# Windowed variance ratio on NHWC rows: 30 duos of raw boxes instead of 28, two of them around the mean, earlier warm-up, rings of two

## The reference

```python
def _gn(v, G=32, eps=1e-05):          # mean and variance of each group of 6 channels over one image
    g = v.reshape(B_, H_, W_, G, C_ // G)
    m = jnp.mean(g, axis=(1, 2, 4), keepdims=True)
    s = jnp.var(g, axis=(1, 2, 4), keepdims=True)
    return ((g - m) / jnp.sqrt(s + eps)).reshape(v.shape)

w0, w1, w2 = (1, 5, 20)
s = box_sum(box_sum(x, 1, w0), 2, w1)                         # sum of 5 along W
num = box_sum(s * s, 3, w2)                                   # sum of 20 along channels
d = box_sum(box_sum(box_sum(x * x, 1, w0), 2, w1), 3, w2)
denum = d * norm[None, :, :, None]                            # norm: how many of the 5 lie inside
ratio = nan_to_num(num / denum, nan=1.0)
```

## Time and profile before

| | |
|---|---|
| median of 3 runs | 393.49 us (393.3, 393.49, 395.51) |
| the profiled execution | 395.41 us, span 393.6 us |
| PE matmul busy | 371.3 us, 94% |
| ACT busy | 277.0 us, 70% |
| DVE busy | 262.5 us, 67% |
| POOL busy | 233.6 us, 59% |
| PE's share of the chain that ended last | 82% |

### The profile page before, as it was taken

How to read it: one execution, slowest core, us unless ns; L and a number is a source line. 1 busy time by engine, 2 the same in 40 slices (tenths; PEclk the granted TensorE clock), 3 DMA queues, 4 the chain that set the end, 5 groups by cost and what they waited for, 6 DMA issues and landing times.

```text
span 393.6 us, 8026 instructions
## 1 busy us (share of the span) xinstructions
PE 371.3 (94%) x3124; PEld 369.7 (94%) x3124; DVE 262.5 (67%) x555; ACT 277.0 (70%) x368; POOL 233.6 (59%) x150
## 2 busy tenths in 40 slices
PE   1999988999999999999889999999999999999982
PEld 1999988999999999999789999999999999999982
DVE  2999952676679999999766455445544455445544
ACT  1455549999999998996447667766777667766751
POOL 4000054887888888886088656765676556765431
PEclk9999989999999999999899999999999999999997
DMA  8999100588988952222203122222211222222213
GB/s 243 327 328 328 57 2 0 162 242 269 292 274 288 296 189 82 81 82 82 80 3 110 50 82 80 82 82 82 80 59 38 66 82 82 80 82 82 80 42 121
DMA packets 66485, 50.84 MB, mean 129 GB/s; under 512 B 912, under 2 KB 66448, under 8 KB 66448
## 3 DMA queue, kind: packets, MB, share of 16 engines
q1 hardware_dynamic: 66448, 50.34, 41.2%
HBM read 25.17 MB, written 25.17 MB: 128 GB/s over the span
## 4 chain that ended last, share of the span: by engine, by line
PE 82%; DVE 6%; issue 4%; ACT 4%; DMA 2%; POOL 0%; DVEq 0%; POOLq 0%; ACTq 0%
PE N L446 20%; PE U L437 19%; PE D L446 16%; PE S L437 16%; PE N L437 5%; PE S L446 4%; DVE late_triples L577 2%; DMA xs<-x 2%; DVE ratio L649 2%; DVE N L652 1%; ACT xs L377 1%; ACT q L395 1%; PE D L500 1%; PE U L521 1%; ACT q L401 1%
## 5 line engine op out<-in xcount | busy, mean ns | idle before, releaser
L318 POOL TENSOR_TENSOR xs<-xs,ratio 128x768 f32<-128x768 f32 x63 | 114.5, 1818 | 91.6 <-DVE ratio L658 91.6
L312 POOL TENSOR_TENSOR xc<-xs,mean_c 128x768 f32<-128x768 f32 x64 | 116.9, 1828 | 60.3 <-DVE mean_c L586 46.2
L649 DVE SCALAR_TENSOR_TENSOR ratio<-D,q 128x768 f32<-128x768 f32 x51 | 48.7, 955 | 91.7 <-ACT q L401 91.7
L652 DVE SCALAR_TENSOR_TENSOR N<-N,q 128x768 f32<-128x768 f32 x64 | 61.6, 963 | 7.5 <-PE N L446 3.9
L658 DVE SCALAR_TENSOR_TENSOR ratio<-ratio,N 128x768 f32<-128x768 f32 x64 | 61.1, 954 | 6.8 <-DVE N L652 0.5
L395 ACT ACTIVATE q<-D 128x768 f32<-128x768 f32 x51 | 41.4, 811 | 30.0 <-PE D L446 30.0
L368 ACT ACTIVATE xs<-S 128x768 f32<-128x768 f32 x36 | 29.2, 811 | 38.7 <-PE S L437 38.7
L401 ACT ACTIVATE q<-q 128x768 f32<-128x768 f32 x64 | 54.0, 844 | 2.0
L437 PE MATMUL U<-b5d,xs 128*128 128x128 f32 x432 | 54.1, 275 | 1.1 <-ACT xs L352 1.1
L437 PE MATMUL S<-b,xc 128*128 128x128 f32 x432 | 54.6, 277 | 0.0
L446 PE MATMUL N<-b_r,xs 128*128 128x138 f32 (+2 forms) x384 | 53.3, 288 | 0.0
(11 more groups left out here) (67 smaller groups left out, 382.2 us busy)
## 6 DMA issues: line engine op xcount, KB each, us to landing
out<-xs SPq DMA_DIRECT2D x31, 768.0 KB, 3.8
xs<-x SPq DMA_DIRECT2D x8, 1536.0 KB, 14.7
xs<-x SPq DMA_DIRECT2D x16, 768.0 KB, 5.4
out<-xs SPq DMA_DIRECT2D x2, 384.0 KB, 2.9
```

The costliest lines, as they stand in the source:

```text
L312: nc.gpsimd.tensor_tensor(pairs(xc[:, n % XC_RING, :]), pairs(x_flat(n)), mean, ALU.subtract)\
L318: nc.gpsimd.tensor_tensor(x_flat(n), x_flat(n), ratio[:, n % RATIO_RING, :], ALU.add)\
L649: nc.vector.scalar_tensor_tensor(t1, in_bank(d_bank(n)), -TINY, pairs(q[:, n % Q_RING, :]), ALU.add, ALU.mult).then_inc(t1_ready, 1)
L652: nc.vector.scalar_tensor_tensor(in_bank(N), in_bank(N), TINY, pairs(q[:, n % Q_RING, :]), ALU.add, ALU.mult).then_inc(t2_ready, 1)
```

## The change

`RAW` becomes 15, so `RAW_DUOS` is 30 and `SWAPPED` is 28, and xs has one more step of room. To make it, the rings of centred rows and of ratios have two buffers instead of three. The first 28 raw boxes (`FIRST_FILL`) are taken as before; duo 28 goes to bank U and duo 29 to bank S, behind the averages. `m2_sum` and the offsets move to banks D and N. `box_u(0)` stands ahead of the average of the squares, `keep_u(0)` ahead of the scaling of the bands. The matmuls that no one reads are sixteen instead of eight, use b5 alone, and stand at the start of the program instead of behind the offsets.

```diff
-RAW = 14
+RAW = 15
 RAW_DUOS = RAW * STEP_DUOS
+
+FIRST_FILL = RAW_DUOS - 2
...
-XC_RING, U_RING, Q_RING, RATIO_RING = 3, 2, 2, 3
+XC_RING, U_RING, Q_RING, RATIO_RING = 2, 2, 2, 2
...
-WARM = 8
+WARM = 16
...
-        m2_sum = [S[:, 0, 0:GROUPS], beside[1][:, 2 * GROUPS:3 * GROUPS]]
-        offsets_wide_ps = S[:, 1, 0:CHUNKS * 128].rearrange("p (j w) -> p j w", j=CHUNKS)
+        m2_sum = [D[:, 0, CHUNKS * 128:CHUNKS * 128 + GROUPS], beside[1][:, 2 * GROUPS:3 * GROUPS]]
+        offsets_wide_ps = N[:, 1, 0:CHUNKS * 128].rearrange("p (j w) -> p j w", j=CHUNKS)
...
+        def raw_bank(n):
+            if n < FIRST_FILL:
+                return (S, N)[n % 2]
+            return (U, S)[n - FIRST_FILL]
...
-            for n in range(RAW_DUOS):
+            for n in range(FIRST_FILL + 1):
                 keep_raw(n)
             act.wait_ge(dev_ready, 1)
             nc.scalar.activation(dev[0], dev[0], ACT.Square).then_inc(dev_squared, 1)
             square_xc(0)
+            keep_raw(FIRST_FILL + 1)
             square_xc(1)
+            keep_u(0)
             act.wait_ge(inv_ready, 1)
...
             ins.then_inc(b20_ready, 1)
-            keep_u(0)
+            keep_u(1)
             square_raw(0)
-            keep_u(1)
             square_xc(2)
...
                 if n:
                     pe.wait_ge(us_ready, n)
+                else:
+                    pe.wait_ge(raw_kept, FIRST_FILL + 1)
                 box5(U, xc2_of(n), b5d).then_inc(u_ready, 1)
...
             pe.wait_ge(bands_ready, 1)
+            keep_warm()
             pe.wait_ge(b5d_ready, 1)
-            for n in range(RAW_DUOS):
+            for n in range(FIRST_FILL):
                 box_raw(n)
...
             average_block(LOADS - 1).then_inc(mean_in_psum, 1)
-            pe.wait_ge(raw_kept, RAW_DUOS)
+            box_raw(FIRST_FILL)
+            pe.wait_ge(raw_kept, FIRST_FILL)
             pe.wait_ge(mean_ready, 1)
             spread_offsets().then_inc(offsets_in_psum, 1)
-            keep_warm()
+            box_raw(FIRST_FILL + 1)
+            box_u(0)
             average_squares(0).then_inc(var_in_psum, 1)
-            box_u(0)
             box_u(1)
...
             dve.wait_ge(mean_in_psum, 1)
-            dve.wait_ge(raw_kept, RAW_DUOS)
+            dve.wait_ge(raw_kept, FIRST_FILL)
...
             mend_edges(0, STEP_DUOS)
+            dve.wait_ge(raw_kept, RAW_DUOS)
             mend_edges(STEP_DUOS, RAW_DUOS - STEP_DUOS)
```

More of the change, by code:

```diff
@@ L175, in d_bank, with raw_bank_free @@
             return S if n < SWAPPED and n % 2 else D
+        def raw_bank(n):
+            if n < FIRST_FILL:
+                return (S, N)[n % 2]
+            return (U, S)[n - FIRST_FILL]
+        def raw_bank_free(n):
+            return max([k + 1 for k in range(n) if raw_bank(k) is raw_bank(n)], default=0)
         def slot(n):
@@ L339, in keep_raw @@
             def keep_raw(n):
-                bank = (S, N)[n % 2]
                 act.wait_ge(raw_in_psum, n + 1)
-                nc.scalar.activation(pairs(raw_box(n)), in_bank(bank), ACT.Copy).then_inc(raw_kept, 1)
+                nc.scalar.activation(pairs(raw_box(n)), in_bank(raw_bank(n)), ACT.Copy).then_inc(raw_kept, 1)
             def square_xc(n):
@@ L454, in box_raw @@
                     pe.wait_ge(loaded0[n // LOAD_DUOS], 16)
-                if n >= 2:
-                    pe.wait_ge(raw_kept, n - 1)
-                box5((S, N)[n % 2], x_flat(n), b5).then_inc(raw_in_psum, 1)
+                if raw_bank_free(n):
+                    pe.wait_ge(raw_kept, raw_bank_free(n))
+                box5(raw_bank(n), x_flat(n), b5).then_inc(raw_in_psum, 1)
             def box_s(n):
@@ L480, in sum_d @@
                 if n == 1:
-                    pe.wait_ge(edges_ready, 2)
+                    pe.wait_ge(raw_kept, RAW_DUOS)
                 box20(d_bank(n), u[:, n % U_RING, :], batch(n)).then_inc(d_ready, 1)
@@ L489, in sum_n @@
                 else:
-                    pe.wait_ge(raw_kept, RAW_DUOS)
+                    pe.wait_ge(edges_ready, 2)
                 if n == MEAN_AT:
@@ L520, in keep_warm @@
                 for _ in range(WARM):
-                    nc.tensor.matmul(U[:, 0, 0:W], b5[:, :], b5d[:, :], start=True, stop=True)
+                    nc.tensor.matmul(U[:, 0, 0:W], b5[:, :], b5[:, :], start=True, stop=True)
             def spread_offsets():
```

## The result

The changed kernel takes 396.69 us (median of 20 runs, 395.03 to 397.90) against 394.44 us for the kernel before (20 runs, 393.17 to 395.51): a ratio of 1.0057, 95% interval 1.0042 to 1.0072. It is slower by a little over half a per cent. The forecast of 393.2 us and its range up to 395.6 us missed; "within 1%" holds.

What follows compares the result with a forecast made beforehand. The prediction took TensorE as the bound in the raw and late loops, busy without a gap. Its terms, -2.7 + 2.85 - 2.1 + 1.7 = -0.25 us, gave 393.2 us against the 393.49 us median; range 390.9 to 395.6 us.

Steps and rivals of the forecast that it cites:

- The two boxes: Raw loop, duos 28 and 29 taken raw: two duos go from 5.58 to 4.23 us, -2.7 us.
- The join: Passage to the second batch: thirteen measures instead of seven stand before the late average while TensorE waits, +2.85 us.
- Rival (b): Measures at the join are hidden because VectorE catches up in duos 26 and 27: 390.4 us, chance 0.06.
- (d): The ring of two for centred rows binds in the late loop, about 33 duos paying: 398 us, chance 0.04.
- (a): TensorE's clock stays up after the 2.0 us gap ahead of box_u(2): 391.5 us, chance 0.26.
- The start, -2.1 us: Load through first mean to box_u(2): earlier by 2.1 us in all, 1.5 of it from the warm-up; bound -0.8.
- The gap ahead of box_u(2), +1.7 us: After the first mean: 2.0 us of idle TensorE in one piece drops its clock to half, +1.7 us; bounds 0 and 1.7.
- The same loss already stands after the join ... taken as nothing: After the join: half clock already costs before, so the longer 4.9 us gap adds 0 to +0.3 us, taken as nothing.
- Rings of two. Cost 0: Raw and late loops: two buffers make centring wait for a later box, with 1.9 us left in the late loop; cost 0.

Runs made afterwards that it cites:

- six: The changed kernel with six measures instead of three behind duos 26 and 27, leaving seven at the join: 395.5 us, ratio 1.0024 to before.
- dropped measures: The changed kernel without the last six of batch 1's 64 measures (statistics wrong), leaving seven at the join: 393.4 us, ratio 0.9964 to before.
- the warm-up alone: The kernel before with sixteen unread matmuls ahead of the first rows, the eight behind the offsets kept: 393.37 us, ratio 0.9989.
- both with rings of two: The kernel before with two buffers for centred rows and ratios (394.82 us, ratio 1.0016), and for centred rows only (393.98 us, one run).
- the run with the wait filled: The changed kernel with 21 unread matmuls while TensorE waits at the join for thirteen measures: 395.45 us, ratio 1.0005 to before.

## Why the prediction was wrong

**Right.** The two boxes: 4.23 us instead of 5.58 in duos 26 and 27, -2.69 us by the table against -2.7. The join: PE waited 4.71 us instead of 1.93, +2.8 against +2.85, with one row of 6.07 us for thirteen measures. I priced both rightly, but did not see that they are one: DVE is the bound in this stretch, so the measures that the two boxes used to cover come out behind them, and the pair brings nothing. Rival (b), in which DVE catches up, fell. So did (d): the late loop keeps 5.57 us a duo with the ring of two. Of (a), the clock that stays up behind the 2.0 us gap came true in about half of the runs, by their group, and the total was 4 us above its figure all the same.

**The start, -2.1 us.** Against the trace that it was worked out from, it was -1.38 us; against an undisturbed execution, -0.18. The reduce came at 50.27, not 49.82: the last average, when it stands alone, takes 0.59 us by its row, not the 0.33 of its pace among others. In my sum ACT's new order had no price, though I had written down that box_u(1) would end at 57.5 and the bands would be ready before; putting the square first gives 0.5 us back. Nor is the 1.1 us of the load a fixed gain of the warm-up: two traces without one have the early reduce too. The larger part is the base: 1.2 us of "gain" was the low clock in this trace of before, which its second trace doesn't have. I had noted that the runs lie 2 us apart and did not ask what in the trace the 2 us are.

**The gap ahead of box_u(2), +1.7 us.** Priced right when it comes (1.65 us), but it comes in some executions only: in one of the two traces of the changed kernel, and in those of six and of dropped measures; not in the other four traces with this gap.

**"The same loss already stands after the join ... taken as nothing".** This step failed. I took the loss for one that before always has, and so left the clock at the join out of the sum. It stands there in some executions of before only. The join's wait of 1.93 to 1.95 us was followed by half clock in three traces (before's first, the warm-up alone, the dropped measures) and not in three (before's second, both with rings of two). And where before had it, it cost 1.1 us at N(31) and not 1.7, since box_u(32) waits for ACT behind it, 1.14 us instead of 1.70. With the wait of 4.71 us the clock fell in all five traces that have it unfilled. The change turned a possible loss into one that every such trace has: 1.7 us between N(28) and N(31), by the run with the wait filled.

**"Rings of two. Cost 0".** I checked the rings in the raw and in the late loop, rightly, and not at the passage, where DVE scales the bands between two passes of N. There the later centring falls into the scaling: +0.64 us.

The sum as measured, from the second trace of before to the first of the changed kernel: -0.18 (start) - 0.02 - 2.69 (boxes) + 2.84 (join) + 1.69 (clock at the join: 0.21 + 1.48) + 0.64 (ring) = +2.28 us. The largest differences to the forecast are 1.9 us at the start and 1.7 us at the join; the gap's +1.7 us was not paid in this execution.

Against the disturbed trace that the forecast was worked out from, the same steps give -1.38 (start) - 0.02 - 2.69 + 2.84 + 0.59 (clock at the join) + 0.65 (ring) = -0.01 us, close to the forecast of -0.25. That is luck: a gap that was not paid makes up for a start, a join and a ring that were priced too low. The -0.25 us was then set on the median of three runs, 393.49, a run of the lower group, though it came from a trace of the upper one, and 20 runs put that median at 394.44. Of the 3.5 us between forecast and result 0.95 is this, the rest are the terms above.

## What to carry to other kernels

When the runs of a kernel fall into groups, find in the traces what separates them before pricing a change against one profile; here a good part was one engine's clock behind waits of 1 to 2 us, and filling three of these waits, with a warm-up, brought more than the change was to bring. Where work is taken off an engine that is always busy, ask what the next engine does in that stretch: if its work is merely moved by the edit, nothing is gained. Check a shorter ring at every irregular place of the program, not only in the steady loops.

## What the runs showed of the hardware

Waits of PE of like length were followed by half clock in some executions and not in others:

| PE's wait, unfilled | traces | with half clock behind or in it |
|---|---|---|
| 0.99 to 1.35 us, ahead of box_u(1), before's order | 6 | 0 |
| 1.03 to 1.35 us, for the last measured block, changed order | 7 | 0 |
| 1.13 us, for the first mean, before's order | 5 | 4 |
| 1.47 to 1.70 us, ahead of box_u(32), and ahead of box_u(2) with the square first | 8 | 0 |
| 1.93 to 1.95 us, at the join | 6 | 3 |
| 2.0 us, ahead of box_u(2) | 7 | 3 |
| 2.49 us, at the join | 1 | 0 |
| 4.71 us, at the join | 5 | 5 |

Both traces of the same unchanged file differ in this, before as well as changed. So the length alone does not decide it below 2.5 us; what does, no run here shows.

VectorE's scaling of the bands, three instructions of 128 x 137 to 147 float32 within SBUF, takes 0.70 us alone and up to 2.30 us beside a GpSimd pass, and ends only behind that pass. The Trainium skill, "GPSIMD Engine Reference", section "Specifications", says that GpSimd shares its SBUF interfaces with VectorE, and that they contend where VectorE works in a two-port mode or reads two inputs from SBUF. The traces show such a contention for this instruction; which of the two conditions holds for it wasn't tried.
